# Shortening the stagger of the output norm in a conv-attention kernel by one step

## The reference, cut to what matters

```python
x = x + conv_part(group_norm(x))          # layer 0, 8 images of 96 x 64 x 64
t = t + attention(layer_norm(t))          # layer 1, tokens of 96 channels
t = t + ffn_fp8(layer_norm(t))

# conv_part, after the selective scan in four directions gave y (192 channels, 4096 places):
y   = layer_norm(y) * on_g + on_b         # over the 192 channels   <- the part changed
y   = y * silu(z)                         # the gate
x1  = inp * skip_scale + y @ out_proj_w.T
x2n = layer_norm(x1)                      # over 96 channels ("ln2")
cb  = conv3x3(gelu(conv3x3(x2n)))         # the two convolutions "cab1", "cab2"
cb  = cb * channel_attention(mean(cb))
out = x1 * skip_scale2 + cb
```

## Time and profile before

| | us |
|---|---|
| median of 3 runs | 11793.42 |
| lowest and highest | 11786.2 and 11815.23 |
| the profiled execution's own time | 11786.2 |
| span in its profile | 11784.4 |
| PE busy | 10415.9 (88% of the span) |
| DVE busy | 10483.9 (89%) |
| ACT busy | 9335.6 (79%) |
| POOL busy | 9496.4 (81%) |
| mean granted clock of TensorE | 0.975 |

### The profile page before, as it was taken

How to read it: one execution, slowest core, us unless ns; L and a number is a source line. 1 busy time by engine, 2 the same in 40 slices (tenths; PEclk the granted TensorE clock), 3 DMA queues, 4 the chain that set the end, 5 groups by cost and what they waited for, 6 DMA issues and landing times. The chain is left out here.

```text
span 11784.4 us, 124896 instructions
## 1 busy us (share of the span) xinstructions
PE 10415.9 (88%) x35584; PEld 4882.5 (41%) x35584; DVE 10483.9 (89%) x7561; ACT 9335.6 (79%) x20418; POOL 9496.4 (81%) x4213
## 2 busy tenths in 40 slices
PE   7989889888898988989889898888988989889898
PEld 3444334443344433444334443344433444334443
DVE  7999789997899978999789997899978999789996
ACT  6888678886788867888678886788867888678886
POOL 5999469994699946999469994699946999469993
PEclk9999999999999999999999999899999999999999
DMA  5777547774477745777457774577745777457773
GB/s 148 224 223 224 121 144 224 224 222 114 149 223 225 223 109 154 224 224 221 105 157 224 223 223 103 159 223 224 222 101 162 222 225 224 98 166 222 227 221 88
DMA packets 673215, 2191.42 MB, mean 186 GB/s; under 512 B 160400, under 2 KB 162448, under 8 KB 661968
## 3 DMA queue, kind: packets, MB, share of 16 engines
q1 hardware_dynamic: 672528, 2183.44, 63.4%
HBM read 2085.75 MB, written 67.44 MB: 183 GB/s over the span
## 5 line engine op out<-in xcount | busy, mean ns | idle before, releaser
L1360 POOL TENSOR_TENSOR state<-state,c_sb 128x1024 f32<-128x1024 f32 x3072 | 7183.9, 2381 | 210.4 <-DMA c_sb<-bc 109.6
L1110 PE MATMUL ps<-state,wt 128*128 128x512 f32 x12288 | 5736.9, 600 | 64.5 <-ACT ya L1181 26.2
L1328 DVE TENSOR_TENSOR_SCAN state<-decay,carry,ps 128x1024 f32<-128x1024 f32 x1728 | 3987.8, 2337 | 41.3 <-issue 6.1
L1110 PEld LDWEIGHTS ps<-state,wt 128*128 128x128 f32 x12288 | 2263.3, 191 | 2253.2 <-issue 1933.2
L1234 ACT ACTIVATE dbu_t<-du_t,b_t 128x128 f32<-128x128 f32 (+1 forms) x10176 | 2951.0, 366 | 25.3 <-PE ps L1101 25.3
L1253 ACT ACTIVATE decay<-delta,a_neg 128x1024 f32<-128x1024 f32 x2304 | 2640.7, 1146 | 0.0
L1349 POOL TENSOR_TENSOR dbu<-b_sb,du 128x1024 f32<-128x1024 f32 x768 | 1822.9, 2374 | 180.1 <-DVE du L1333 157.3
L1315 DVE TENSOR_TENSOR ps<-ps,du 128x1024 f32<-128x1024 f32 x1288 | 1554.6, 1207 | 40.0 <-PE ps L1055 39.9
L1188 ACT COPY carry<-state 128x1 f32<-128x1 f32 x3072 | 568.2, 185 | 1250.9 <-DVE state L1328 1234.9
L1055 PE MATMUL ps<-parts,sel 114*128 114x512 bf16 (+1 forms) x2576 | 794.5, 391 | 791.2 <-DVE state L1328 790.1
L1328 DVE TENSOR_TENSOR_SCAN state<-ps,carry,dbu 128x1024 f32<-128x1024 f32 x576 | 1347.6, 2340 | 110.8 <-POOL dbu L1349 93.3
(11 more groups left out here) (227 smaller groups left out, 9633.2 us busy)
## 6 DMA issues: line engine op xcount, KB each, us to landing
c_sb<-bc SPq DMA_DIRECT2D x2048, 512.0 KB, 4.6
c_sb<-bc SPq DMA_DIRECT2D x2048, 256.0 KB, 5.9
b_sb<-bc SPq DMA_DIRECT2D x512, 512.0 KB, 3.9
b_sb<-bc SPq DMA_DIRECT2D x512, 256.0 KB, 4.0
gates<-gate_a SPq DMA_DIRECT2D x8, 2048.0 KB, 6.8
x_tok<-x SPq DMA_DIRECT2D x256, 48.0 KB, 1.8
gn<-gn_t SPq DMA_DIRECT2D x8, 1536.0 KB, 7.1
gate_a<-gates SPq DMA_DIRECT2D x8, 1536.0 KB, 10.6
```

What stands on the lines that cost most here:

```text
L1110: mm = pe.matmul(py[:, q * CH:(q + 1) * CH], col("ident"), state[:, slot(g, n), q * CH:(q + 1) * CH], start=(n == 0), stop=False)
L1328: dve.tensor_tensor_scan(state[:, slot(g, n), way], rate, what, 0.0 if fresh else carry[:, n:n + 1], ALU.mult, ALU.add)\
L1360: pool.tensor_tensor(state[:, slot(g, n), :], state[:, slot(g, n), :], c_sb[:, n % CRING, :], ALU.mult).then_inc(S["weighted"], 1)
```

## The change

The variance matmul of chunk j, which stood two iterations after `fold(j)`, is now written inside `fold(j + 1)`, right behind its matmuls (the last one has a place of its own in the next iteration). The root on ACT moves from lag 2 to lag 1, and everything behind it, down to the last layer norm, by one as well. The two border rows of `cpad` are cleared behind all eight adds of POOL instead of behind the fifth. `cab1` gets two banks of its own (those of `yr1` and `on_mean1`), and its first chunk waits for all eight `on_center` in the place of the last two `yr_copy`; the banks of `sum0` and `sum1` move with it.

```diff
-CAB1_AT, SUM_AT, CAB2_AT, CA_AT, X2_AT = 9, 13, 19, 23, 26
+CAB1_AT, SUM_AT, CAB2_AT, CA_AT, X2_AT = 8, 12, 18, 22, 25
...
-            bank.update(cab1_0=bank["yr0"], cab1_1=bank["yr1"], sum0=bank["on_mean0"], sum1=bank["on_mean1"])
-            bank.update(cab2_0=bank["on_var"], cab2_1=bank["out"], ca1=bank["ln2_mean"], ca2=bank["ln2_var"])
+            bank.update(cab1_0=ps[3][0], cab1_1=ps[3][1])
+            bank.update(zip(("sum0", "sum1", "cab2_0", "cab2_1", "ca1", "ca2"), sum(ps, [])))
...
                         pe.matmul(mean, col("ones_di"), y5[:, sl(j)], start=False, stop=True)\
                           .then_inc(S["on_mean_mm"], 1)
+                        if j > 0:
+                            var_192(j - 1)
...
                         if j == 0:
                             pe.wait_ge(S["back_in"], 64)
                             pe.wait_ge(S["cpad_zero"], 2)
-                        if j < 2:
-                            pe.wait_ge(S["yr_copied"], NCH - 1 + j)
+                            pe.wait_ge(S["on_centered"], NCH)
...
-                    staggered((0, fold), (2, var_192), (4, out_proj),
+                    staggered((0, fold), (1, lambda j: var_192(j) if j == NCH - 1 else None), (3, out_proj),
...
-                              (2, lambda j: ln_root(act, j, bank["on_var"], S["on_var_mm"], rs, S["on_log"],
+                              (1, lambda j: ln_root(act, j, bank["on_var"], S["on_var_mm"], rs, S["on_log"],
                                                     S["on_rsqrt"], 128)),
...
                         pool.tensor_tensor(sqa[0:DR, sl(j)], sqa[0:DR, sl(j)], sqr[:, sl(j)], ALU.add)\
                             .then_inc(S["sq_added"], 1)
-                        if j == 4:
-                            pool.wait_ge(S["gated"], 1)
-                            pool.memset(cpad[:, 0:1, :], 0.0).then_inc(S["cpad_zero"], 1)
-                            pool.memset(cpad[:, H + 1:H + 2, :], 0.0).then_inc(S["cpad_zero"], 1)
+                    pool.wait_ge(S["gated"], 1)
+                    pool.memset(cpad[:, 0:1, :], 0.0).then_inc(S["cpad_zero"], 1)
+                    pool.memset(cpad[:, H + 1:H + 2, :], 0.0).then_inc(S["cpad_zero"], 1)
...
-                    staggered((0, on_center), (3, on_unit), (3, gate), (4, skip),
+                    staggered((0, on_center), (2, on_unit), (2, gate), (3, skip),
```

More of the change, by code:

```diff
@@ L1501, in kv_sum @@
                             mm.then_inc(S["kvt_mm"], 1)
-                    staggered((0, fold), (2, var_192), (4, out_proj),
-                              (5, lambda j: ln_sum(pe, j, x1, S["x1_ready"], bank["ln2_mean"], S["ln2_centered"],
+                    staggered((0, fold), (1, lambda j: var_192(j) if j == NCH - 1 else None), (3, out_proj),
+                              (4, lambda j: ln_sum(pe, j, x1, S["x1_ready"], bank["ln2_mean"], S["ln2_centered"],
                                                    S["ln2_mean_mm"])),
-                              (6, lambda j: ln_sum(pe, j, sq2, S["ln2_squared"], bank["ln2_var"], S["ln2_log"],
+                              (5, lambda j: ln_sum(pe, j, sq2, S["ln2_squared"], bank["ln2_var"], S["ln2_log"],
                                                    S["ln2_var_mm"])),
@@ L1622, in _ @@
                     staggered((0, yr_copy), (0, on_square),
-                              (2, lambda j: ln_root(act, j, bank["on_var"], S["on_var_mm"], rs, S["on_log"],
+                              (1, lambda j: ln_root(act, j, bank["on_var"], S["on_var_mm"], rs, S["on_log"],
                                                     S["on_rsqrt"], 128)),
-                              (5, lambda j: ln_square(act, j, cen2, S["ln2_centered"], sq2, S["ln2_squared"])),
-                              (6, lambda j: ln_root(act, j, bank["ln2_var"], S["ln2_var_mm"], rs2, S["ln2_log"],
+                              (4, lambda j: ln_square(act, j, cen2, S["ln2_centered"], sq2, S["ln2_squared"])),
+                              (5, lambda j: ln_root(act, j, bank["ln2_var"], S["ln2_var_mm"], rs2, S["ln2_log"],
                                                     S["ln2_rsqrt"])),
-                              (7, ln2_affine), (SUM_AT + 1, gelu), (CAB2_AT + 1, cab2_out),
+                              (6, ln2_affine), (SUM_AT + 1, gelu), (CAB2_AT + 1, cab2_out),
                               (CA_AT, lambda j: mean_out() if j == 0 else None),
@@ L1766, in weigh @@
                                                  ALU.mult, ALU.add).then_inc(S["x2_ready"], 1)
-                    staggered((0, on_center), (3, on_unit), (3, gate), (4, skip),
-                              (5, lambda j: ln_center(dve, j, x1, bank["ln2_mean"], S["ln2_mean_mm"], cen2,
+                    staggered((0, on_center), (2, on_unit), (2, gate), (3, skip),
+                              (4, lambda j: ln_center(dve, j, x1, bank["ln2_mean"], S["ln2_mean_mm"], cen2,
                                                       S["ln2_centered"])),
-                              (6, skip2),
-                              (7, lambda j: ln_unit(dve, j, cen2, rs2, S["ln2_rsqrt"], cen2, S["ln2_unit"])),
+                              (5, skip2),
+                              (6, lambda j: ln_unit(dve, j, cen2, rs2, S["ln2_rsqrt"], cen2, S["ln2_unit"])),
                               (CAB1_AT + 1, sides), (SUM_AT + 2, hidden_sum),
```

## The result

| | before | after |
|---|---|---|
| median, us | 11793.56 | 11921.26 |
| lowest to highest | 11786.2 to 11815.23 | 11917.71 to 11923.95 |
| span of the profiled execution | 11784.4 | 11919.8 |
| mean granted clock | 0.975 | 0.969 |

The ratio is 1.0103, 95% interval 1.0091 to 1.0115; it rests on more executions (23 of the changed kernel) than the table's medians, which give 1.0108. The forecast was 11885, range 11842 to 11912: the direction is right, the size is not, and the time lies outside the range. The waits came nearly as worked out. What the lower clock costs, at the new waits and at old ones, was priced at about a third of what it is.

The account below looks back on a forecast made before the run. The stage was taken as bound by PE up to cab1; 8 x (8.4 waits + 2.3 clock behind cab1(0) + 0.7 clock in first iterations) = 91 us on 11786.2, median 7.2 higher: 11885, range 11842 to 11912.

Parts of the forecast that it names:

- A delay before cab1 is carried on in full: PE delay before cab1 persists to the first cab2, as image 4's 1.71 us did.
- The loop: Variance, root, copy, centre, squares, POOL's add, next variance now form a closed circle of 6.28 to 6.87 us, taken as 6.77.
- The first iterations and cab1(0): PE waits 3.2, 1.3 and 0.4 us before variance(1) to (3), 5.5 before cab1(0): +8.4 us an image.
- The clock behind cab1(0): Lower granted clock over 7 us behind the new 5.5 us wait: 2.3 us an image, bounds 0 and 3.1.
- The clock in the first iterations: Lower clock behind the new 3.2 us wait before variance(1): 0.7 us an image, bounds 0 and 1.7.
- Behind cab1(0): 0: After cab1(0) PE's rows are the same and the old waits of 1.19 and 1.70 stay: 0 us.
- The sum: 8 x (8.4 + 2.3 + 0.7) = 91 us over the whole kernel.
- Rival 1: Same waits before and at cab1(0), but the clock costs nothing: 56 to 70 us, about 11860; chance 0.17.
- rivals 2 to 5: Pipeline fills sooner, 11757 (0.04); loop-bound iterations, 11899 (0.10); delay absorbed later, 11793 (0.04); half the cab1(0) wait, 11825 (0.05).
- rival 3: Full iterations become bound by the loop, grown beyond 7.24 us to, say, 7.8: 14 us more, 11899; chance 0.10.

Follow-up runs that it names:

- e5: Changed kernel with filling matmuls whose results are unused, six in front of cab1(0) and three behind fold(2): 11881.29 us, ratio 1.006.
- e4: Changed kernel with six filling matmuls on PE in the wait in front of cab1(0), results unused: 11887.25 us, ratio 1.0074.
- E6: Kernel before with one more unused matmul (0.86 us) in front of cab1(0) in each image: 11823.87 us, ratio 1.0016.
- e8: Kernel before with cab1's new banks, the wait for eight centres and the late clears, lags as before: 11810.05 us, ratio 1.0001.
- e3: Changed kernel with clears behind the fifth add again and the root behind copy and squares on ACT: 11821.52 us, ratio 1.0018.

## Why the prediction was wrong

- *A delay before cab1 is carried on in full*: right. From the first cab1 on the two kernels have the same waits.
- *The loop*: right. Root to copy 1.25 us (1335.29 - 1334.04), the loop 6.86, 6.26 and 6.79 where the clock is full (e5; forecast 6.77 each), wait before variance(1) 3.15 us (3.2).
- *The first iterations and cab1(0)*: right to 0.4 us. Forecast 55.18 us from first fold to first cab1, measured 54.8 at full clock; the wait 5.36 for 5.5, of which the clears 2.5 (2.7). Of the 1.3 us forecast before variance(2) 0.48 came (e5), since POOL's add ahead of it took 1.26 us and not 1.75. Times 8 the waits cost 64 us; forecast 67.
- *The clock behind cab1(0)*: right in kind and nearly in size: 2.7 us (e4) for 2.3. Granted clock over the 7 us between 0.62 and 0.65 in all images.
- *The clock in the first iterations*: this term was mis-sized. The prediction took 0.7 us, because "variance(1) behind it is on the loop, the folds are not". At half clock variance, out_proj and fold of an iteration take not 5.5 but about 10 us, more than the loop, so where the clock stayed low PE itself was the bound (10.10 us, above). Over the images low clock cost 465.2 / 8 - 54.8 = 3.4 us in this part, before 382.1 / 8 - 46.8 = 1.0: 2.4 instead of 0.7. The spread is wide: behind the new wait four images lost 3.7 to 3.8 us, two 0.7 to 0.9 and two nothing, 2.1 in the mean. The rest comes from the old wait of 2.37 at the stage's start, behind which the clock fell in 6 of 8 images instead of 4.
- *Behind cab1(0): 0*. This is the step that failed. The prediction said "so the waits of 1.19 and 1.70 stay: 0". They did stay as waits, but a wait had a second price, which the profile before showed and I passed over: image 3 lost 1.7 us behind the one of 1.70, where the other seven lost nothing. After the change all 8 do (4.43 above), and the attention part loses 2.9 in 7 of 8 images and 1.5 in the last, where 2 of 8 did. Together 32.6 + 16.4 - 8 x 2.7 = 27 us, and 0 was forecast. E6 showed that 0.86 us of shift is enough to bring these drops on. The two go together: of the 96 images in the twelve traces 41 have a drop behind the third cab1_sum's wait, and in 40 of these the clock falls again at the start of the attention part; of the other 55 it does so in 16.
- *The sum*: 64 + 8 x (2.4 + 2.7) + 27 = 132 of 135.4 us; the rest lies in the scan, which also varies between the runs.
- Rival 1 (no clock cost) and rivals 2 to 5 did not come: of rival 3 the low clock in the first iterations did, but the full iterations kept their 7.24 us (1363.29 - 1356.05). The range was built from clock bounds at the new waits alone, and so ended at 11912.

What stays open: why in the changed kernel all 8 images come to the old waits at the moment that costs. The low stretch behind cab1(0) began 1.4 to 2.0 us before it in all 8 images, so they are in step from there, but how they come into step was not tried. By e8's counts a part of the 27 us may also be that the profiled execution of before had few drops. Which wait the drops in the attention part follow is open too, since no run filled one there.

## What to carry to other kernels

Shortening the distance between two steps of a software pipeline also reorders each engine's list: look for a step that now stands ahead of the one it indirectly waits for, since it closes a loop that was open (here root(j-1) ahead of yr_copy(j)). And where a kernel has waits of one to two microseconds on TensorE, look whether the clock falls behind some of them in some loop passes: here a shift of their moment by 0.86 us changed the time by 0.16%, 0.06% of it the added matmul. So price a change with the losses at old waits in the range, and compare two versions by the same stretch at full clock. Even there look at the waits: in the kernel before that stretch was 46.8 us each time, in e3 it ran from 47.9 to 49.9.

## What the runs showed of the hardware

The same wait of 1.70 us was followed by a stretch at the lower clock in 1 of 8 images before, in 2 of 8 in e8 with the same waits, in 8 of 8 after, in 7 of 8 with 0.86 us of shift. Filling the wait of 5.36 us with 5.3 us of useless matmuls made the kernel faster by 34 us (e4). At the lower level two fp32 records of 512 columns take 1.7 to 1.9 us instead of 0.86.
